# A second early SAGE sweep over three blocks with the late unit's own product made ahead, and a triangle product of the edge build replaced by sums of ranks on TensorE

## The chip, the cores and the metric

The kernel runs on one core of a Trainium2 chip, in one launch. The time is the device time of that core in microseconds (us). TensorE (PE) multiplies matrices into PSUM, VectorE (DVE) and ScalarE (ACT) work element by element, GpSimd (POOL) here mainly issues indirect DMAs, and SyncE (SP) issues the large DMAs. PEld is the loading of weights into TensorE, beside its matmuls. Lower is better.

## The reference

Four graph networks over the same 6250 nodes and 100000 edges (`src`, `dst`, sorted by `dst`), each with a residual and a layer norm. Cut to what matters:

```python
def aggregate(m, w): return segment_sum(m[src] * w[:, None], dst, 6250)

# L0: GCN, 3 layers, edge weights w and self loops, norm = dinv[src] * w * dinv[dst]
h = relu(gcn(x, W1, b1)); h = relu(gcn(h, W2, b2)); x = layernorm(x + gcn(h, W3, b3) @ Wl + bl)
# L1: SAGE, 2 layers: mean over the incoming edges
h = relu(x @ W1_self + mean_agg(x) @ W1_neigh + b1)
x = layernorm(x + h @ W2_self + mean_agg(h) @ W2_neigh + b2)
# L2: encoder, 5 steps of a GRU over aggregate(h @ conv_w[i], 1), decoder
x = layernorm(x + decoder(gru5(encoder(x))))
# L3: GCN with unit weights, 1 layer
x = layernorm(x + gcn(x, W, b))
```

## The kernel before

The kernel makes two dense adjacency matrices in HBM, source node by destination node (6272 x 6272): `W_adj` in float32 with the edge weights, for the first network, and `C_adj` in float16 with edge counts, for the others. Each aggregation is then a dense product of node features with such a matrix.

**Build** (`build_adjacency`). SP writes zeros over both matrices. The edges come in 49 batches of 2048 (16 tiles of 128). Two edges of one batch can be the same cell, so each batch is first merged: for each tile pair (j, i) with j <= i a 128x128 matrix `Eq` tells which edge of tile j has the key of which edge of tile i. DVE makes the `Eq` rows of the first 6 tiles (`compare_rows`, L474), ACT those of the other 10 from a squared distance and a Relu (`distance` L306, `equality` L314), each with the row sums in `total`. ACT also issues the loads of the batch's keys (`load_keys`, L291): the one for batch b+2 after its own rows of batch b, and after DVE's (`row_used`). DVE then makes one-hot matrices for the degrees (`one_hots`: L482, L487, L497) and `Et`, the diagonal blocks of `Eq` times a triangle (row <= column), in two halves (L495, L500). TensorE's `batch` waits for `equal_set` (the last of these) and `late_rows` (ACT's), multiplies all `Eq` blocks by the weights and a count (L554), each `Et` block by a column of ones (L557), and the one-hots (L560), and counts `batch_counted`. DVE's `merge` (L508 to L517) takes the sums from PSUM: an edge is the last of its cell if no equal one is at or after it (`total` minus the triangle's sum is 0); its target is the cell then, and a spare place otherwise. DVE's order is: compare rows of batch b+1, merge batch b, one-hots of batch b+1. POOL adds one tile per indirect DMA (`add_column`, L606), 784 for `W_adj` and then 784 for `C_adj`, in the batches' order, each batch after its `cell_set`.

**Layers** (`run_layers`). A stage (start, gcn 0 to 2, sage, enc, gru 0 to 3, out) aggregates the features it makes: 13 blocks of 512 destination nodes, in four sweeps over all 49 chunks of 128 source nodes. A sweep (first block, blocks, first PSUM bank) holds its blocks in PSUM banks, and for each chunk SP loads the matrix rows of these blocks into a ring of 8 slots (one more for chunk 0), up to 8 ahead of TensorE (`chunk_used`); `chunk` (L1049) multiplies one block after the other, in two passes either way (float32, or a high and a low half in float16). The start stage and gcn 2 take the blocks downwards, `DOWNWARD = ((9,4,0), (5,4,4), (1,4,0), (0,1,4))`, since the edges of the last blocks are added first. Before their last sweep, over block 0 alone, comes the head of the next stage's aggregation. For gcn 2 that is the sage stage with `EARLY_SWEEPS["sage"]`: of its first two sweeps the first 1 + 5 x 8 = 41 chunks (`early_parts`, `EARLY_LAPS`), whose source nodes are all outside unit 0. Their units (4 chunks each) have their dense part made as they come: `sage_products` (L1070 own, L1071 neighbour), `sage_unit` on DVE, `sage_turned` (L1080), with the PSUM banks of `SAGE_BANKS`. The late unit, unit 0, is made after gcn 2's last sweep, then the 8 remaining chunks of both sweeps follow, and the other two sweeps.

SP waits before sweep k of the start stage and of gcn 2 until the adds which that sweep's blocks need have landed (`ready`), and before their last sweep until all 784 of that matrix have (`adds_landed`); nothing queued on SP behind that wait is loaded sooner. This point is called the **gate** below, once for `W_adj` and once for `C_adj`. The lines for it are those in `sync` of `run_layers` under `if added:`.

## Time and profile before

| | us |
|---|---|
| median of 3 runs (5269.39 to 5279.17) | 5274.72 |
| the profiled execution, its own time | 5281.61 |
| its span, first to last instruction | 5279.8 |
| PE busy in the span | 4749.6 (90%) |
| POOL busy in the span | 2490.1 (47%) |
| the chain that ended last: PE / DVE / issue / DMA | 83% / 10% / 3% / 3% |

The build takes the first 988 us or so of the span and the layers the rest. In the build no engine is busy all the time on its own page line; what bounds it is read from one batch of the timeline. In the layers TensorE hardly ever waits. POOL's adds go on beside both until about 3021 us. The rows that the prediction reads are below, in groups.

### The profile page before, as it was taken

Reading aid. Unit: us, or ns where it says so; the run is one execution under the profiler, and the core shown is the slowest. Engines: PE = TensorE matmul, PEld = TensorE weight load, DVE = VectorE, ACT = ScalarE, POOL = GpSimd, SP = SyncE. Lnnn points to the kernel's source line nnn. Section 1 sums busy time; section 2 is a strip of 40 time slices with the busy share of each in tenths; the row PEclk is TensorE's granted clock in tenths of the full one; section 3 lists DMA queues with packets and bytes.
Section 4 is the critical chain, followed back from the end, with each engine's and each line's share of the span. In section 5 each row is a group of like instructions: output and inputs, shape, how many; then the busy total and the mean of one; then the engine's idle time right before and its main releaser. Section 6 shows DMA issues by size and latency. Waiting matters only on the chain.

```text
span 5279.8 us, 74661 instructions
## 1 busy us (share of the span) xinstructions
PE 4749.6 (90%) x25659; PEld 2552.1 (48%) x25659; DVE 1671.3 (32%) x3025; ACT 1364.8 (26%) x2522; POOL 2490.1 (47%) x1708
## 2 busy tenths in 40 slices
PE   3555555799999999999999999999999999999999
PEld 3555555444444444444455444544444444444444
DVE  9999999400000000110051103203022030220642
ACT  7898998300000111111120002102011020110410
POOL 4788888888888888888888700000000000000100
PEclk7665555799999999999999999999999999999999
DMA  9999998599999999999999986785866858768477
GB/s 327 342 340 340 329 338 217 138 309 307 289 279 293 291 297 287 287 279 299 257 253 274 265 302 195 233 284 163 292 216 217 287 168 282 229 205 287 141 238 249
DMA packets 792328, 1402.59 MB, mean 266 GB/s; under 512 B 268308, under 2 KB 513000, under 8 KB 760808
## 3 DMA queue, kind: packets, MB, share of 16 engines
q1 hardware_dynamic: 552012, 1342.89, 76.9%
q0 software_dynamic: 225792, 0.70, 7.9%
q10 hardware_dynamic: 14364, 56.99, 2.9%
q8 instruction: 84, 1.38, 0.1%
q14 instruction: 76, 0.62, 0.0%
HBM read 1160.09 MB, written 240.26 MB: 265 GB/s over the span
## 4 chain that ended last, share of the span: by engine, by line
PE 83%; DVE 10%; issue 3%; DMA 3%; ACT 0%; SPq 0%; ACTq 0%; DVEq 0%
PE psum L1049 66%; DVE arena L474 5%; PE psum L560 3%; DMA arena<-W_adj 2%; PE psum L554 2%; PE psum L997 2%; PE psum L999 2%; DVE arena L495 1%; PE psum L1004 1%; PE psum L1001 1%; DVE arena L500 1%; DVE arena L482 1%; DVE arena L497 1%; PE psum L1097 1%; PE psum L981 1%
## 5 line engine op out<-in xcount | busy, mean ns | idle before, releaser
L1049 PE MATMUL psum<-arena 128*128 128x512 f16 (+3 forms) x14014 | 3668.7, 422 | 18.5 <-DMA arena<-W_adj 10.4
L1049 PEld LDWEIGHTS psum<-arena 128*128 (+2 forms) x14014 | 1670.3, 123 | 1958.7 <-issue 866.2
L606 POOL DMA_INDIRECT W_adj<-arena x784 | 1216.1, 1551 | 272.3 <-issue 242.6
L606 POOL DMA_INDIRECT C_adj<-arena x784 | 1218.8, 1555 | 241.3 <-issue 241.3
L857 POOL TENSOR_TENSOR arena<-arena 128x512 f32 (+1 forms) x13 | 21.7, 1673 | 1693.3 <-DVE arena L1630 1693.3
L554 PE MATMUL psum<-arena 128*128 (+1 forms) x6664 | 226.4, 167 | 433.5 <-DVE arena L500 398.3
L474 DVE TENSOR_SCALAR_CACHE_REDUCE arena<-arena 128x2048 bf16<-128x2048 f32 (+5 forms) x294 | 572.0, 2007 | 0.0
L306 ACT ACTIVATE arena<-arena 128x1280 bf16<-128x1280 f32 (+4 forms) x490 | 426.7, 880 | 95.4 <-PE psum L560 45.1
L554 PEld LDWEIGHTS psum<-arena 128*128 128x128 bf16 x6664 | 215.1, 104 | 448.2 <-issue 401.3
L314 ACT ACTIVATE arena<-arena 128x1280 bf16<-128x1280 bf16 (+4 forms) x490 | 424.2, 866 | 0.0
L1892 DVE COPY arena<-psum 128x512 f32<-128x512 f32 (+1 forms) x39 | 23.2, 653 | 1009.9 <-PE psum L1097 1009.9
L560 PE MATMUL psum<-arena 128*128 128x98 f32 x1568 | 307.7, 386 | 2.0 <-issue 1.8
L1894 DVE TENSOR_SCALAR arena<-psum,arena 128x512 f32<-128x512 f32 (+1 forms) x31 | 22.2, 735 | 903.0 <-PE psum L1049 903.0
L560 PEld LDWEIGHTS psum<-arena 128*128 128x128 f32 x1568 | 300.6, 299 | 2.4 <-issue 2.3
L1547 ACT ACTIVATE arena<-psum,arena 128x512 f32<-128x512 f32 (+1 forms) x47 | 28.2, 650 | 931.7 <-PE psum L1049 931.7
L1527 ACT ACTIVATE arena<-arena 128x128 f32 x288 | 85.4, 308 | 516.1 <-PE psum L1049 502.3
L855 POOL COPY arena<-arena 128x512 f32 (+1 forms) x13 | 8.0, 616 | 326.2 <-DVE arena L1630 326.2
L997 PE MATMUL psum<-arena 128*128 (+1 forms) x260 | 137.4, 611 | 9.9 <-DVE arena L1901 5.9
L1516 ACT ACTIVATE arena<-arena 128x128 f32<-128x128 f32 x4 | 0.9, 297 | 546.9 <-DVE arena L1685 546.9
L999 PE MATMUL psum<-arena 128*128 (+1 forms) x260 | 134.5, 599 | 0.0
L1773 DVE SCALAR_TENSOR_TENSOR arena<-psum,arena 128x512 f32 (+1 forms) x48 | 36.0, 751 | 293.5 <-ACT arena L1426 293.5
L557 PE MATMUL psum<-arena 128*128 128x1 bf16 x784 | 126.0, 165 | 2.1 <-issue 2.1
(269 smaller groups left out, 2589.4 us busy)
## 6 DMA issues: line engine op xcount, KB each, us to landing
arena<-C_adj SPq DMA_DIRECT2D x653, 384.0 KB
arena<-C_adj SPq DMA_DIRECT2D x441, 512.0 KB
arena<-W_adj SPq DMA_DIRECT2D x196, 1024.0 KB
arena<-W_adj SPq DMA_DIRECT2D x163, 768.0 KB
arena<-C_adj SPq DMA_DIRECT2D x294, 288.0 KB
arena<-W_adj SPq DMA_DIRECT2D x98, 832.0 KB
W_adj<-arena SPq DMA_DIRECT2D x24, 3200.0 KB
W_adj<-arena SPq DMA_DIRECT2D x24, 3072.0 KB
```

The lines of the kernel that those rows point to most:

```text
L306: act.activation(apart[:, u % 2, 0:(TB - j) * P], krow[:, slot, j * P:], ACT.Square, bias=keyf[:, b * TB + j:b * TB + j + 1], scale=-1.0). ...
L314: act.activation(Eq[:, slot, at:at + (TB - j) * P], apart[:, u % 2, 0:(TB - j) * P], ACT.Relu, bias=one[:, 0:1], scale=-1.0, accum_out=tot ...
L474: ins = dve.tensor_scalar(Eq[:, slot, at:at + (TB - j) * P], krow[:, slot, j * P:], keyf[:, b * TB + j:b * TB + j + 1], None, ALU.is_equal ...
L482: dve.tensor_tensor(high, psRamp[:, 0:CHUNKS].unsqueeze(1).to_broadcast([P, TB, CHUNKS]), dhi[:, b * TB:(b + 1) * TB].unsqueeze(2).to_broa ...
L554: pe.matmul(psS[:, slot, 5 * i:5 * i + 4], Eq[:, slot, block_of(j, i)], V[:, ds(b * TB + j, 1), :].rearrange("p a c -> p (a c)"), start=(i ...
L557: pe.matmul(psS[:, slot, 5 * i + 4:5 * i + 5], Et[:, slot, own_at(i), :], ones[:, 0:1], start=False, stop=(i == TB - 1), skip_group_check= ...
L560: ins = pe.matmul(psD[:, 0:2 * CHUNKS], ohl[:, j, :], ohv[:, slot, j].rearrange("p c k -> p (c k)"), start=False, stop=False, skip_group_c ...
L606: return pool.indirect_dma_start(table, bass.IndirectOffsetOnAxis(idx[:, t:t + 1], 0), values[:, of:of + 1], None, compute_op=ALU.add)
L997: pe.matmul(psum[:, banks[gate], :], gates[:, gate * D:(gate + 1) * D], unit(fm, j), start=True, stop=False)
L999: pe.matmul(psum[:, banks[gate], :], wt[f"whhT{gate}"], unit(h_fm, j), start=False, stop=True).then_inc(s["probs_in"], 1)
L1049: ins = pe.matmul(psum[:, bank + b, 0:width], lhs, ring[:, slot, offset + b * BANK:offset + b * BANK + width], start=begin and part == 0, ...
L1527: act.activation(chunk32[:, u, :], h_nm[:, ds(i * LAP + (u + 1), 1), :].rearrange("p a f -> p (a f)"), ACT.Copy).then_inc(s["chunk_set"], 1)
```

## The change

**Build.** The triangle's product is gone: `psUpto`, `Et`, `own_at` and DVE's two multiplications L495 and L500 per batch. In place of the column of ones against `Et`, TensorE now multiplies the diagonal block of `Eq` itself by `rank` (two columns: ones, and a power of two that grows with the partition). The first sum counts the equal edges of the own tile, the second compares with `above`, 1.875 times the own power, which tells whether an equal edge stands later in the tile. DVE's merge gets one more operation of 16 columns (`later`), so `merged` counts 4 per batch, and its setup 7 small operations in place of one. `equal_set` is now signalled by the weighted one-hot.

**Early SAGE sweep.** The second early sweep goes over three blocks, 2 to 4, in banks 5 to 7, in place of two, 3 and 4, in banks 6 and 7; the stage's last sweep goes over two blocks in place of three. The late unit's own product (`late_product`, 4 matmuls) is made in the first early sweep, after chunk place 20, into bank 6; DVE copies it to `own_in`, the second early sweep waits for the copy (`late_kept`), and after the gate only the neighbour products of the late unit are left.

```diff
-SAGE_BANKS = (((0, 1, 2),), ((4, 5, 6),), ((5, 6, 7),), ((4, 5, 4),))
+SAGE_BANKS = (((0, 1, 2),), ((4, 5, 6),), ((5, 6, 7),), ((4, 6, 4),))
...
-EARLY_SWEEPS = {"gcn": ((5, 4, 0), (9, 4, 4), (2, 3, 0), (0, 2, 4)), "sage": ((5, 4, 0), (3, 2, 6), (9, 4, 0), (0, 3, 4))}
+EARLY_SWEEPS = {"gcn": ((5, 4, 0), (9, 4, 4), (2, 3, 0), (0, 2, 4)), "sage": ((5, 4, 0), (2, 3, 5), (9, 4, 0), (0, 2, 4))}
...
@@ build_adjacency: scalar
-                act.wait_ge(s["merged"], 3 * (b - 3) + 1)
+                act.wait_ge(s["merged"], 4 * (b - 3) + 1)
@@ build_adjacency: vector, setup
-        dve.memset(ones, 1.0)
+        dve.memset(rank[:, 0:1], 1.0)
...
-        link(dve.tensor_scalar(psUpto, ramp, pcol[:, 0:1], None, ALU.is_ge))
+        link(dve.tensor_copy(place[:, 0:1], pcol))
+        link(dve.tensor_scalar(place[:, 1:2], place[:, 0:1], 1, None, ALU.logical_shift_right))
+        link(dve.tensor_tensor(place[:, 0:1], place[:, 0:1], place[:, 1:2], ALU.add))
+        link(dve.tensor_scalar(place[:, 0:1], place[:, 0:1], float(RANK_LOW), None, ALU.add))
+        link(dve.tensor_scalar(power.bitcast(I32), place[:, 0:1], 23, None, ALU.logical_shift_left))
+        dve.tensor_copy(rank[:, 1:2], power)
+        link(dve.tensor_scalar(above, power, RANK_EDGE, None, ALU.mult))
@@ one_hots
-            dve.wait_ge(s["late_rows"], b * (TB - DVE_ROWS) + half - DVE_ROWS)
-            dve.tensor_tensor(Et[:, slot, 0:half, :], near, psUpto.unsqueeze(1).to_broadcast([P, half, P]), ALU.mult)
             dve.wait_ge(s["hot_set"], b + 1)
             dve.tensor_tensor(weighted, high, psW[:, b * TB:(b + 1) * TB].unsqueeze(2).to_broadcast([P, TB, CHUNKS]),
-                              ALU.mult)
-            dve.wait_ge(s["late_rows"], (b + 1) * (TB - DVE_ROWS))
-            dve.tensor_tensor(Et[:, slot, half:, :], far, psUpto.unsqueeze(1).to_broadcast([P, half, P]),
                               ALU.mult).then_inc(s["equal_set"], 1)
@@ merge
-            dve.tensor_scalar(mask, more, 0.0, -1.0, ALU.is_equal, ALU.mult).then_inc(s["merged"], 1)
+            dve.scalar_tensor_tensor(out=later, in0=sums[:, :, 5], scalar=above[:, 0:1], in1=more, op0=ALU.is_ge,
+                                     op1=ALU.add).then_inc(s["merged"], 1)
+            dve.wait_ge(s["merged"], 4 * b + 2)
+            dve.tensor_scalar(mask, later, 0.0, -1.0, ALU.is_equal, ALU.mult).then_inc(s["merged"], 1)
@@ build_adjacency: tensor
-                pe.matmul(psS[:, slot, 5 * i + 4:5 * i + 5], Et[:, slot, own_at(i), :], ones[:, 0:1],
+                pe.matmul(psS[:, slot, 6 * i + 4:6 * i + 6], Eq[:, slot, block_of(i, i)], rank,
                           start=False, stop=(i == TB - 1), skip_group_check=True)
@@ run_layers: tensor
+            def late_product(j, ahead):
+
+                pe.wait_ge(s["products_read"], ahead.read + early_units().index(j))
+                for c in range(UC):
+                    ins = pe.matmul(psum[:, sage_banks(j)[1], c * D:(c + 1) * D],
+                                    h_fm[:, j * BANK + c * P:j * BANK + (c + 1) * P], wt["W1s"], start=True, stop=True)
+                ins.then_inc(s["late_own"], 1)
...
                             if i_:
+                                pe.wait_ge(s["late_kept"], 1)
                                 pe.wait_ge(s["seconds_read"], ahead.seconds + early_units().index(units[-1]) + 1)
...
+                                if i_ == 0 and place == UC * (len(units) + 1):
+                                    late_product(early_units()[-1], ahead)
                                 early_spell(place, ahead, ("sage", 0), i_)
@@ run_layers: vector, sage_unit and gcn 2
+                if j in early_units_of(SPLIT):
+                    own = own_in[:, 0].rearrange("p (c f) -> p c f", f=D)
+                    dve.wait_ge(s["late_kept"], 1)
...
+                        if sweep == SPLIT:
+                            dve.wait_ge(s["late_own"], 1)
+                            dve.tensor_copy(own_in[:, 0], psum[:, sage_banks(early_units()[-1])[1], :]) \
+                                .then_inc(s["late_kept"], 1)
```

How the instructions stand in the program, first on DVE in the build: the end of a batch's comparisons, the merge of the batch before, the one-hots, and the next comparison. Before:

```order
L474 TENSOR_SCALAR arena<-arena 128x1408
L508 TENSOR_REDUCE arena<-psum 128x16
L509 CAST arena<-psum 128x16
L510 SCALAR_TENSOR_TENSOR arena<-psum,arena 128x16
L513 TENSOR_SCALAR arena<-arena 128x16
L515 TENSOR_TENSOR arena<-arena 128x16
L517 TENSOR_TENSOR arena<-arena 128x16
L482 TENSOR_TENSOR arena<-psum,arena 128x16x49
L487 TENSOR_TENSOR arena<-psum,arena 128x2048
L495 TENSOR_TENSOR arena<-arena,psum 128x1024
L497 TENSOR_TENSOR arena<-arena,psum 128x16x49
L500 TENSOR_TENSOR arena<-arena,psum 128x1024
```

The same place in the changed kernel, where lines are numbered anew (L478 is the comparison, L508 the new operation, L486, L491 and L495 the one-hots):

```order
L478 TENSOR_SCALAR arena<-arena 128x1408
L503 TENSOR_REDUCE arena<-psum 128x16
L504 CAST arena<-psum 128x16
L505 SCALAR_TENSOR_TENSOR arena<-psum,arena 128x16
L508 SCALAR_TENSOR_TENSOR arena<-psum,arena 128x16
L511 TENSOR_SCALAR arena<-arena 128x16
L513 TENSOR_TENSOR arena<-arena 128x16
L515 TENSOR_TENSOR arena<-arena 128x16
L486 TENSOR_TENSOR arena<-psum,arena 128x16x49
L491 TENSOR_TENSOR arena<-psum,arena 128x2048
L495 TENSOR_TENSOR arena<-arena,psum 128x16x49
```

The two operations of 1024 columns are gone and one of 16 columns came. Next, TensorE from the fourth unit of the early SAGE work to the first chunks after the gate. Before (L1049 is `chunk`, L1070 and L1071 own and neighbour product, L1080 the transposes):

```order
L1080 MATMUL psum<-arena 128x128 x4
L1049 MATMUL psum<-arena 128x512 x462
L1070 MATMUL psum<-arena 128x128
L1071 MATMUL psum<-arena 128x128
L1070 MATMUL psum<-arena 128x128
L1071 MATMUL psum<-arena 128x128
L1070 MATMUL psum<-arena 128x128
L1071 MATMUL psum<-arena 128x128
L1070 MATMUL psum<-arena 128x128
L1071 MATMUL psum<-arena 128x128
L1049 MATMUL psum<-arena 128x512 x32
```

In the changed kernel (L1047 is `chunk`, L1077 the late unit's own product, L1070 the neighbour product, L1087 the transposes):

```order
L1087 MATMUL psum<-arena 128x128 x4
L1047 MATMUL psum<-arena 128x512 x32
L1077 MATMUL psum<-arena 128x128 x4
L1047 MATMUL psum<-arena 128x512 x512
L1070 MATMUL psum<-arena 128x128 x4
L1047 MATMUL psum<-arena 128x512 x32
L1087 MATMUL psum<-arena 128x128 x4
```

Between the last transposes of the early units and the late unit's neighbour product stand 544 chunk matmuls where 462 stood, 82 more, and the own product moved up among them. Last, SP over the same stretch, before:

```order
L898 DMA arena<-C_adj 128x2048 x41
L898 DMA arena<-C_adj 128x1024 x41
L881 DMA arena<-C_adj 128x512
L934 DMA arena<-C_adj 128x3x512 x16
L881 DMA arena<-C_adj 128x2048 x8
```

and in the changed kernel:

```order
L896 DMA arena<-C_adj 128x2048 x41
L896 DMA arena<-C_adj 128x1536 x41
L879 DMA arena<-C_adj 128x512
L932 DMA arena<-C_adj 128x3x512 x16
L879 DMA arena<-C_adj 128x2048 x8
```

The 41 loads ahead of the gate carry three blocks in place of two. The gate is SP's wait ahead of the load of 512 columns.

## Rows read from the trace of the kernel before

**Rows 1.** The page: TensorE's busy tenths in 40 slices of the span.

```profile
PE   3555555799999999999999999999999999999999
```

**Rows 2.** Timeline of one batch: start, us, engine, line, operation, idle before and releaser.

```profile
417.45 2.34 DVE L474 TENSOR_SCALAR_CACHE_REDUCE arena<-arena 128x2048 bf16<-128x2048 f32 x1
...
423.01 5.62 PE L560 MATMUL psum<-arena 128*128 128x98 f32 x32
...
429.04 0.20 DVE L508 TENSOR_REDUCE arena<-psum 128x16 f32<-128x48 f32 x1
...
435.05 1.21 DVE L500 TENSOR_TENSOR arena<-arena,psum 128x1024 bf16<-128x1024 bf16 x1
...
436.18 2.34 DVE L474 TENSOR_SCALAR_CACHE_REDUCE arena<-arena 128x2048 bf16<-128x2048 f32 x1
...
436.65 0.18 PE L554 MATMUL psum<-arena 128*128 x1 [8.03 <-DVE arena L500]
```

**Rows 3.** View of line L474: durations in ns, first and last start.

```profile
L474 DVE TENSOR_SCALAR_CACHE_REDUCE arena<-arena x294: 1669/2008/2348, 28.4 to 965.5; 128x2048 bf16<-128x2048 f32 x49, 128x1792 bf16<-128x1792 f32 x49, 128x1536 bf16<-128x1536 f32 x49
```

**Rows 4.** Waits from 300 to 900 us: us in total, times, longest.

```profile
PE psum L554 <- DVE arena L500: 242.0, 31, 8.2
```

**Rows 5.** Timeline of ACT: first rows of batches 1 and 2.

```profile
40.54 2.51 ACT L306 ACTIVATE arena<-arena 128x1280 bf16<-128x1280 f32 x2 [3.63 <-DVE arena L474]
...
58.70 2.51 ACT L306 ACTIVATE arena<-arena 128x1280 bf16<-128x1280 f32 x2 [0.54 <-ACT arena L314]
```

**Rows 6.** Timeline: TensorE's end of the build and first chunks of the layers.

```profile
980.02 6.94 PE L560 MATMUL psum<-arena 128*128 128x98 f32 x32
...
995.35 15.17 PE L1049 MATMUL psum<-arena 128*128 128x512 f32 x35 [4.89 <-ACT arena L1436]
...
999.75 0.34 PEld L1049 LDWEIGHTS psum<-arena 128*128 128x128 f32 x1 [0.52 <-issue]
...
1001.11 0.19 PEld L1049 LDWEIGHTS psum<-arena 128*128 128x128 f32 x1 [0.24 <-issue]
```

**Rows 7.** Timelines of POOL, TensorE and SP about the gate of W_adj.

```profile
1551.65 1.55 POOL L606 DMA_INDIRECT W_adj<-arena  x1 [0.30 <-issue]
...
1555.01 114.32 PE L1049 MATMUL psum<-arena 128*128 128x512 f32 x266
...
1600.28 0.37 SPq L881 DMA_DIRECT2D arena<-W_adj  x1
```

**Rows 8.** Timelines of the same engines about the gate of C_adj.

```profile
2979.70 73.33 PE L1049 MATMUL psum<-arena 128*128 128x512 f16 x339
...
3019.43 1.56 POOL L606 DMA_INDIRECT C_adj<-arena  x1 [0.30 <-issue]
...
3025.44 0.36 SPq L881 DMA_DIRECT2D arena<-C_adj  x1
...
3053.72 0.49 PE L1070 MATMUL psum<-arena 128*128 128x128 f32 x2 [0.69 <-ACT arena L1547]
...
3055.60 0.59 PE L1049 MATMUL psum<-arena 128*128 128x512 f16 x2
```

**Rows 9.** Timeline of POOL: the start of batch 2's adds.

```profile
141.55 0.19 POOL L580 TENSOR_TENSOR arena<-arena 128x1 f32<-128x1 f32 x1 [14.02 <-issue]
```

**Rows 10.** DMA issues by transfer: KB each, median us from issue to landing.

```profile
keys<-arena ACTq DMA_DIRECT2D x1, 392.0 KB, 2.3
...
W_adj<-arena SPq DMA_DIRECT2D x1, 16.0 KB, 5.2
```

**Rows 11.** Timeline of ACT at the end of the sage stage.

```profile
3209.86 1.26 ACT L1547 ACTIVATE arena<-psum,arena 128x512 f32<-128x512 f32 x2 [62.19 <-PE psum L1049]
```

**Rows 12.** Timeline of SP: loads of the second early sweep, two blocks each.

```profile
2999.97 25.36 SPq L898 DMA_DIRECT2D arena<-C_adj  x30
```

**Rows 13.** POOL's adds by line, from 300 to 900 us and from 1600 to 3000 us.

```profile
L606 POOL DMA_INDIRECT W_adj<-arena x319 | 493.8, 1548 | 101.9 <-issue 98.3 <-DMA W_adj<-arena 3.4 <-DVE arena L517 0.2
...
L606 POOL DMA_INDIRECT C_adj<-arena x746 | 1159.4, 1554 | 230.1 <-issue 230.1
```

More of the change, by code:

```diff
@@ L44 @@
 ZONES = 36
+RANK_LOW = 32
+RANK_EDGE = 1.875
 ZONE = 256
@@ L190, in build_adjacency @@
     psD = psum[:, 3, :]
-    psRamp, psUpto = psum[:, 2, 0:P], psum[:, 2, P:2 * P]
+    psRamp = psum[:, 2, 0:P]
     psW = psum[:, 4:6, :].rearrange("p a b -> p (a b)")[:, 0:TILES]
@@ L212, in build_adjacency @@
     V = take(P, [TILES, 4], BF16)
-    ones, one = take(P, [16], BF16), take(P, [8], F32)
+    rank, one = take(P, [2], BF16), take(P, [8], F32)
+    power, above, place = take(P, [1], F32), take(P, [1], F32), take(P, [2], I32)
     ramp = take(P, [P], F32)
@@ L216, in build_adjacency @@
     krow = take(P, [2, B], F32)
-    Et = take(P, [2, TB, P], BF16)
     ohl, ohv = take(P, [TB, P], F32), take(P, [2, TB, 2, CHUNKS], F32)
-    total, more = take(P, [3, TB], F32), take(P, [TB], F32)
+    total, more, later = take(P, [3, TB], F32), take(P, [TB], F32), take(P, [TB], F32)
     apart = take(P, [2, (TB - DVE_ROWS) * P], BF16)
@@ L505, in merge @@
             dve.wait_ge(s["batch_counted"], b + 1)
-            sums = psS[:, slot, 0:TB * 5].rearrange("p (i c) -> p i c", c=5)
+            sums = psS[:, slot, 0:TB * 6].rearrange("p (i c) -> p i c", c=6)
             at = slice(b * TB, (b + 1) * TB)
@@ L531, in vector @@
         dve.wait_ge(s["ramps"], 7 + SPLIT)
-        dve.tensor_copy(ones, ones).then_inc(built, 1)
+        dve.tensor_copy(rank, rank).then_inc(built, 1)
     def tensor(pe):
@@ L789, in run_layers @@
             "sum_dve sum_act hi_set var_set std_set gates_set pre_set new_set unit_set kept dve_step " \
-            "dve_stage act_stage abs_set reach_in reach_set probs_in probs_set " \
+            "late_own late_kept dve_stage act_stage abs_set reach_in reach_set probs_in probs_set " \
             "enc_in enc_set enc_out enc_kept parts_in " \
```

16 lines of the change are left out of this document (6 added, 10 removed).

## The prediction

> **What bounds the kernel now.** The page's line of busy tenths comes first: from the ninth slice on TensorE is busy nine tenths or more [rows 1], so the layers are bound by TensorE, and only the build, before it, and places where TensorE comes to wait can give time. I then read one batch of the build in the timeline. From DVE's first comparison at 417.45 to the next one at 436.18 are 18.7 us without a gap, and TensorE stands for 8.0 us until L500 ends [rows 2]. Comparisons run from the first at 28.4 to the last at 965.5, and the last of a batch starts some 10 us after its first: 927 us for 48 batches, 19.3 us a batch [rows 3]. DVE bounds the build, with TensorE close beside it: its idle time is 242.0 us in 31 batches or 7.8 us each [rows 4], so it works 11.5 us of 19.3.
>
> The third thing to read is a clock of its own. POOL's adds go at one pace from the start of batch 2 at 141.55 [rows 9] to the last at 3019.43 [rows 8], and neither DVE's work nor TensorE's sets them. All of `W_adj` must have landed before the start stage's last sweep and all of `C_adj` before gcn 2's. SP got past the first gate at 1600.28, 47 us after POOL's last add of `W_adj` ended at 1553.2 [rows 7], and past the second at 3025.44, 4.4 us after the last add ended at 3020.99 [rows 8]. So the first gate has room, and the second has nearly none. Whatever is won in the build reaches the second gate and stops there, unless other work stands ahead of it. That is how I price the change.
>
> **The build.** Removed: L495 and L500, 1.21 us each (the row is of L500, and the other has its shape) [rows 2]. Added: one operation of 16 columns, which I take at the 0.2 us of L508 [rows 2]. DVE's own turn falls from 18.7 to 18.7 - 2.4 + 0.2 = 16.5 us. Next is the turn through TensorE: 11.5 us of matmuls, 0.5 us from DVE's signal to the first of them (436.18 to 436.65), and DVE's part outside the comparisons, which was 436.18 - 429.04 = 7.1 and becomes 4.9 us [rows 2]: 16.9 us. But late is now ACT. It makes ten rows of each batch and sends for keys in between, and at the start, where nobody held it, batch 1 to batch 2 took 58.70 - 40.54 = 18.16 us with only its own work before it [rows 5]. In the kernel before that was hidden under 19.3. So the batch falls to 18.2 and not to 16.9. ACT's chain: 40.5 + 47 x 18.16 = 894.0 for its start of batch 48, with a later start of some 1 us (seven small setup operations on DVE ahead of the first comparison) against 1 us for the two key loads that the last batches lack. Its rows take 18.16 - 0.54 = 17.6, TensorE's batch then 11.5 to 12: 923.5, where it was 980.02 + 6.94 = 986.96 [rows 6]. The build ends **63 us** sooner. The ends are 0 (the removed operations hidden after all) and 48 x (19.3 - 16.9) = 115 us. I take 63 since it comes from a row in which ACT runs alone. TensorE's matmuls cost nothing new: as many, two columns wide for one, on weights of the same size. The keys come denser by 6%, beside SP's zeros; POOL's batch 2 waits for zeroed cells [rows 9], and for one more key load of 1 MB ahead of it I allow 1 us on the whole of POOL's stream, 0 to 3 as the range.
>
> **From the build to the second gate.** Start stage and gcn stages hold the same work and start at 995.35 - 63 = 932. At the first gate SP arrives at 1537, before the adds have landed, and waits some 18 us. TensorE would begin its last sweep at 1669.33 - 98 x 0.43 = 1627.2 before (49 chunks of two records in the row of 266 [rows 7]), thus at 1564 now; a load issued at about 1555 lands in 2.3 us, or 5.2 at the most [rows 10]. TensorE hardly waits, but it has lost the lead of its ring. Some us may go there, and they cost nothing as long as the second gate is still shut.
>
> At the second gate TensorE began gcn 2's last sweep at 3053.03 - 98 x 0.2163 = 3031.8 (98 of the 339 records in 73.33 us [rows 8]). Ahead of it now stand 41 x 2 = 82 matmuls more, 82 x 0.2163 = **17.7 us**, and the late unit's own product, half of the 1.9 us from 3053.72 to 3055.60 in which both products ran [rows 8]: 0.9 us. TensorE gets there at 3031.8 - 63 + 17.7 + 0.9 = 2987. The added waits `late_own` and `late_kept` hold nothing: DVE has finished its units by then, its copy is one operation of 512 columns, and TensorE has 21 chunks of work until it needs it; behind DVE's wait stands only the sum of that sweep.
>
> The gate opens between 3021.0 (POOL's last add issued) and 3025.4 (SP had passed) [rows 8]. I take 3024, as the adds have still to be made in memory, and 1 us for POOL's later start. SP's issue and its landing take 0.4 and 2.3 us [rows 8, 10]: TensorE starts at **3027.7** after 40 us of idleness. The same point of work lay at 3031.8 + 17.7 + 0.9 = 3050.4 before. Won: 22.7 us.
>
> **Behind the gate.** TensorE resumes at its lower clock: in rows 6 a weight load follows every 0.86 us at 999.75 and every 0.43 us at 1001.11, so from 995.35 it ran 5 us at 1.2 GHz and lost 2.6 us after a wait. I take 3 us, with the empty ring in it; the range is 2.5 to 10. The stage's last sweep has two blocks, so ACT scales one sum there and not two in 1.26 us before the next stage can begin [rows 11]: 0.6 us won. The 82 matmuls come off that sweep (98 of them) and 16 go to the remaining chunks; the sum of work is the same.
>
> **The sum:** 22.7 - 3 + 0.6 = 20.3 us. Against the profiled execution's own 5281.61 that is 5261.3. It lay 6.9 us above the median of the runs, 5274.7, which gives 5254.4: I say **5254 us**.
>
> A rule of the Trainium skill speaks of POOL's stream. The trace first: an add takes 1548 ns in the build, with both removed operations running, and 1554 ns from 1600 to 3000 us, where DVE is nearly idle [rows 13]. "SBUF — State Buffer", section "Who interferes with whom", says that VectorE and GpSimd share a port pair, and that a GpSimd DMA's descriptors wait while DVE holds it. By that rule fewer DVE operations would open the gate sooner; by the rows DVE cost POOL nothing, and the same page exempts an operation with one input in SBUF. The sum keeps 3024.
>
> **The rivals.**
> (a) *The gate does not bind, the build's gain is small.* It decides below 22.7 us of gain at the gate, a batch above 18.8 us; or with over 40 us lost at the first gate with the emptied ring. At 19.0 us a batch the gain is about 13, less little, so 5262. Against it: ACT's 18.16 and 40 us in hand.
> (b) *The two-block sweep is starved.* SP would need 1.3 us for each 256 KB, as in a three-block sweep of six matmuls at 0.2163; decides above 1.27 us a load: 49 x (1.3 - 0.865) = 21 us lost, the gain gone, 5275. Against it: 30 such loads in 25.36 us, 0.85 each, TensorE fed, with POOL's adds beside them [rows 8, 12].
> (c) *Slower: the clock stays low.* After 40 us without work TensorE runs at 1.2 GHz and, fed chunk by chunk from an empty ring, does not get back. Each us of full-speed work costs one more. It decides above 23.3 + 10.5 = 34 us of such work, that is through gcn 2's last sweep (21.2 us) and the 8 four-block chunks behind it (64 x 0.2163 = 13.8). With the three-block ones too (10.4) it is 45 us: 5281.6 - 23.3 + 45 = 5303, at the median 5296. Against it: 5 us in rows 6, also from an empty ring.
> (d) *POOL's stream ends sooner*, the Trainium skill's rule as a mechanism here: adds that waited behind L495 and L500, up to 49 x 2.4 = 119 us. Then TensorE at 2987 binds, 63 + 0.6 us are won: 5211. Against it: rows 13.
>
> **How the numbers follow.** Forecast 0.80, with 12 to 28 us won: 22.7 + 3 + 0.6 and 1 to 2 more at its best, 22.7 - 1.4 (gate at 3025.4) - 2.9 (landing 5.2) - 2 (POOL) - 5 (clock) and so 12 at its worst. (a) 0.08, (b) 0.04, (c) 0.04, (d) 0.04. The runs shown differ by 5 us from their median; the range is 5243 to 5267, and leaves out (b), (c), (d) and parts of the edges. A measurement can tell about 0.2%, 10.5 us. Faster by more: 0.80 + 0.06 of (a) + (d) = 0.90. Within it: 0.06, from (a) and (b). Slower: 0.04.
>
> **What the profile after would show.** The batches every 18.2 us, ACT without idle time but for its key loads, and TensorE waiting for ACT's L-line of `equality` and not for DVE. The first chunk near 932. SP idle at the first gate until about 1555 and TensorE not. One wait of TensorE near 2987 to 3028, ended by a load of `C_adj`, and a granted clock of half for about 5 us behind it. POOL's last add within 3 us of 3019.4. Wrong it would be if that last add moved by more than 10 us, if TensorE did not wait at the second gate, or if the idle time moved to another stage.

## The result, and the profile after

The changed kernel takes 5256.93 us (median of 8 runs, 5255.05 to 5263.43) against 5274.27 us for the kernel before (8 runs beside it, 5269.39 to 5279.17): a ratio of 0.9967 with a 95% interval of 0.9957 to 0.9976. The forecast was 5254 us, its range 5243 to 5267. Its profiled execution took 5257.21 us by its own time, 5255.4 us of it the span.

The build first. These are TensorE's waits over the whole of after (us in total, times, longest), its last three batches of the build, and the first chunk of the layers; below them DVE's comparison line with its first and last start.

```profile
PE psum L552 <- ACT arena L312: 324.1, 42, 8.5
...
882.73 5.93 PE L558 MATMUL psum<-arena 128*128 128x98 f32 x32
...
900.91 7.04 PE L558 MATMUL psum<-arena 128*128 128x98 f32 x32
...
918.44 6.81 PE L558 MATMUL psum<-arena 128*128 128x98 f32 x32
...
934.28 36.16 PE L1047 MATMUL psum<-arena 128*128 128x512 f32 x96 [4.65 <-ACT arena L1446]
...
L478 DVE TENSOR_SCALAR_CACHE_REDUCE arena<-arena x294: 1668/2006/2347, 28.8 to 904.0; 128x2048 bf16<-128x2048 f32 x49, 128x1792 bf16<-128x1792 f32 x49, 128x1536 bf16<-128x1536 f32 x49
```

TensorE waits for ACT's L312 (`equality`, L314 before) where it waited for DVE's L500 [rows 4]. A batch takes 900.91 - 882.73 = 18.2 us, the last one, whose ACT part has no keys to send for, 17.5. The build ends at 925.25 where it ended at 986.96 [rows 6], and the layers begin 61 us sooner.

Now the second gate, in the timelines of TensorE, SP and POOL of after:

```profile
2939.81 45.49 PE L1047 MATMUL psum<-arena 128*128 128x512 f16 x210
...
3019.71 1.56 POOL L604 DMA_INDIRECT C_adj<-arena  x1 [0.30 <-issue]
...
3022.66 0.33 SPq L879 DMA_DIRECT2D arena<-C_adj  x1
...
3024.73 1.03 PE L1047 MATMUL psum<-arena 128*128 128x512 f16 x2 [39.43 <-DMA arena<-C_adj]
3026.80 22.85 PE L1047 MATMUL psum<-arena 128*128 128x512 f16 x96 [1.04 <-DMA arena<-C_adj]
```

POOL's last add comes at 3019.71, where it came at 3019.43 [rows 8]. TensorE is there at 2985.3, stands idle for 39.4 us, and ends gcn 2's last sweep at 3049.65; before it ended at 3053.03. So of 61 us, 3.4 are left here, and the rest of the gain is work that no longer stands behind this point: 82 matmuls and the late unit's own product. At the sage stage's end the two kernels are 22.5 us apart (ACT's last scaling of a sum at 3187.38, 3209.86 in rows 11, one in place of two):

```profile
3187.38 0.69 ACT L1557 ACTIVATE arena<-psum,arena 128x512 f32<-128x512 f32 x1 [41.04 <-PE psum L1047]
```

This reads as the forecast had it. The experiments show that two of its terms were nevertheless wrong.

### The profile page after: what moved, and what is told of

Read it like the earlier page. It is cut to its first block, busy times and chain, and to the rows that moved or that the text cites. A ratio compares the mean times of both kernels' runs of the same rounds, so it can differ in the third digit from the quotient of the medians.

```text
span 5255.4 us, 74620 instructions
## 1 busy us (share of the span) xinstructions
PE 4736.0 (90%) x25659; PEld 2544.5 (48%) x25659; DVE 1574.6 (30%) x2983; ACT 1364.6 (26%) x2522; POOL 2486.5 (47%) x1708
## 4 chain that ended last, share of the span: by engine, by line
PE 42%; POOL 30%; issue 8%; DVE 0%; POOLq 0%; DMA 0%; ACT 0%; ACTq 0%; SPq 0%; DVEq 0%
PE psum L1047 33%; POOL C_adj L604 22%; POOL W_adj L604 8%; PE psum L995 2%; PE psum L997 2%; PE psum L1002 1%; PE psum L999 1%; PE psum L1027 0%; POOLq L598 0%; POOL arena L578 0%; PE psum L975 0%; PE psum L1142 0%; PE psum L1158 0%; PE psum L979 0%; PE psum L1138 0%
## 5 line engine op out<-in xcount | busy, mean ns | idle before, releaser
L1047 PE MATMUL psum<-arena 128*128 128x512 f16 (+3 forms) x14014 | 3670.3, 422 | 55.0 <-DMA arena<-C_adj 40.5
L1047 PEld LDWEIGHTS psum<-arena 128*128 (+2 forms) x14014 | 1670.5, 123 | 1996.2 <-issue 867.5
L604 POOL DMA_INDIRECT W_adj<-arena x784 | 1214.3, 1549 | 273.9 <-issue 245.4
L604 POOL DMA_INDIRECT C_adj<-arena x784 | 1216.8, 1552 | 241.7 <-issue 241.7
L478 DVE TENSOR_SCALAR_CACHE_REDUCE arena<-arena 128x2048 bf16<-128x2048 f32 (+5 forms) x294 | 571.9, 2006 | 0.0
L552 PE MATMUL psum<-arena 128*128 (+1 forms) x6664 | 211.1, 166 | 388.4 <-ACT arena L312 324.1
L312 ACT ACTIVATE arena<-arena 128x1280 bf16<-128x1280 bf16 (+4 forms) x490 | 424.2, 866 | 0.0
L995 PE MATMUL psum<-arena 128*128 (+1 forms) x260 | 137.6, 611 | 9.9 <-DVE arena L1918 5.9
L997 PE MATMUL psum<-arena 128*128 (+1 forms) x260 | 134.6, 599 | 0.0
L555 PE MATMUL psum<-arena 128*128 128x2 bf16 x784 | 126.0, 165 | 0.0
```

Source lines behind the costliest of these rows:

```text
L312: act.activation(Eq[:, slot, at:at + (TB - j) * P], apart[:, u % 2, 0:(TB - j) * P], ACT.Relu, bias=one[:, 0:1], scale=-1.0, accum_out=tot ...
L478: ins = dve.tensor_scalar(Eq[:, slot, at:at + (TB - j) * P], krow[:, slot, j * P:], keyf[:, b * TB + j:b * TB + j + 1], None, ALU.is_equal ...
L552: pe.matmul(psS[:, slot, 6 * i:6 * i + 4], Eq[:, slot, block_of(j, i)], V[:, ds(b * TB + j, 1), :].rearrange("p a c -> p (a c)"), start=(i ...
L555: pe.matmul(psS[:, slot, 6 * i + 4:6 * i + 6], Eq[:, slot, block_of(i, i)], rank, start=False, stop=(i == TB - 1), skip_group_check=True)
L604: return pool.indirect_dma_start(table, bass.IndirectOffsetOnAxis(idx[:, t:t + 1], 0), values[:, of:of + 1], None, compute_op=ALU.add)
L995: pe.matmul(psum[:, banks[gate], :], gates[:, gate * D:(gate + 1) * D], unit(fm, j), start=True, stop=False)
```

## The experiments

In the runs below L604, L605, L606, L609 and L616 are the line of POOL's adds, and L1047 to L1067 that of the sweeps' matmuls. "Last add" is the start of the last add into `C_adj`.

### The two halves apart (e1_build, e2_sweep)

e1_build is the kernel before with the rank sums alone:

```diff
-            dve.tensor_tensor(Et[:, slot, 0:half, :], near, psUpto..., ALU.mult)
...
-            dve.tensor_tensor(Et[:, slot, half:, :], far, psUpto..., ALU.mult)
...
-                pe.matmul(psS[:, slot, 5 * i + 4:5 * i + 5], Et[:, slot, own_at(i), :], ones[:, 0:1],
+                pe.matmul(psS[:, slot, 6 * i + 4:6 * i + 6], Eq[:, slot, block_of(i, i)], rank,
...
+            dve.scalar_tensor_tensor(out=later, in0=sums[:, :, 5], scalar=above[:, 0:1], in1=more, ...)
```

> The kernel before with the rank sums in the build alone; the early sage sweep, the last sweep and the late unit stay as before. Second gate (the stream of adds is a clock of its own, and the wait for the last add into C_adj binds): the build's last matmul comes about 62 us sooner (925 us in place of 987), TensorE then waits at the last sweep of gcn 2 for about 60 us in place of next to none, the last chunks start with the adds at 3020 to 3025 us, and the whole is won by the old slack alone: 3 to 5 us, about 5270 us. Rival (the build's gain passes): 60 us less, about 5212 us. Rival (the small sums matter, no gate): anything between, with no wait of TensorE at C_adj.

e2_sweep is the kernel before with the sweep and the late product alone:

```diff
-..."sage": ((5, 4, 0), (3, 2, 6), (9, 4, 0), (0, 3, 4))}
+..."sage": ((5, 4, 0), (2, 3, 5), (9, 4, 0), (0, 2, 4))}
...
+            def late_product(j, ahead):
...
+                                if i_ == 0 and place == UC * (len(units) + 1):
+                                    late_product(early_units()[-1], ahead)
```

> The kernel before with the second early sage sweep over three blocks and the late unit's own product made ahead; the build stays as before. Second gate: TensorE reaches the last sweep of gcn 2 about 18 us later than before, after the adds have landed, so that nothing is waited for there, and the moved work is merely done earlier: 0 to 2 us won (5272 to 5275 us), the same time. Rival (the reordering is worth something by itself, for example shorter chains at the sage stage's end): 10 us or more. The two halves alone then add up to 3 to 7 us where the change as a whole won 17 to 24.

Measured: e1_build 5281.16 us (11 runs, ratio to before 1.0013, 1.0004 to 1.0022); e2_sweep 5255.3 us (6 runs, ratio 0.9966, 0.9954 to 0.9978). Both expectations missed. The build's half was to win 3 to 5 us and wins nothing: its median lies 5.6 us above that of before beside it. The rival by which its gain passes the gate is refuted, since TensorE waits there for 56.9 us (about 60 expected). The sweep's half wins the whole 20 us by itself, and I had expected 0 to 2. Both expectations stood on the forecast's second sentence on the gate, that TensorE came there at 3031.8 with nearly no room. TensorE at the gate, in e1_build and in e2_sweep:

```profile
3022.96 1.04 PE L1047 MATMUL psum<-arena 128*128 128x512 f16 x2 [56.86 <-DMA arena<-C_adj]
...
3021.92 1.03 PE L1049 MATMUL psum<-arena 128*128 128x512 f16 x2 [13.11 <-DMA arena<-C_adj]
```

e2_sweep has the build of before and 18.6 us more work ahead of the gate, and yet TensorE comes there 23 us sooner than before's profile shows, and waits. So the profile of before was perhaps not what the kernel usually does. (e2_sweep holds both the three-block sweep and the late unit's own product; no run separates the two, 17.7 and 0.9 us in the prediction's sum.)

### A second profile of before (e7_before), and shifted code (e6_shift)

> The kernel before once more, unchanged, for a second profile. If the 81 gaps of TensorE in the build (34.5 us) belong to the program, they are there again and the build ends at 987 us; if they belong to one execution, the build ends about 40 us sooner, TensorE waits 25 to 30 us at C_adj, and the whole is 3 to 5 us shorter than the first profiled run's 5281.6.

e6_shift:

```diff
+SHIFT = 16
...
         pe.transpose(psR, needed, ident[0:NB, 0:NB]).then_inc(s["needed_turned"], 1)
+        for _ in range(SHIFT):
+            pe.wait_ge(s["needed_set"], 2)
```

> The kernel before with 16 waits that are already met put on TensorE's queue ahead of the build's loop; nothing else is changed, and the place of every later instruction of TensorE in its instruction memory is. It asks why the same code of the build took TensorE to 987 us in the profiled run of before and to about 948 us in e2_sweep. If the place of the loop's instructions does it, the idle time of TensorE put down to issue in the build (34.5 us in 81 gaps before, 2.4 us in e2_sweep) changes with the shift, and the build ends up to 40 us sooner; by the second gate the whole then stays within 5 us of before (5270 to 5280), since TensorE only waits longer at C_adj. If it is something else, the profile shows the 81 gaps again.

The waits of TensorE and DVE from 0 to 1000 us, first in the profile that the forecast used, then in e7_before, the same kernel:

```profile
PE psum L554 <- DVE arena L500: 398.3, 48, 26.5
PE psum L554 <- issue: 34.5, 81, 7.6
...
DVE arena L508 <- PE psum L560: 21.3, 26, 1.9
```

```profile
PE psum L554 <- DVE arena L500: 425.7, 49, 26.5
...
DVE arena L508 <- PE psum L560: 13.8, 3, 11.4
```

In the first execution TensorE's stream of small matmuls had 81 gaps that no semaphore explains, so that in 26 batches DVE waited for TensorE. DVE stands idle for 27 of the 937 us from 28 to 965 there, and for 8 of the 915 us from 28 to 943 in e7_before. In e7_before the gaps are absent but for one, DVE's last comparison starts at 943.9 and not at 965.5 [rows 3], and this is the end of the build, the first chunk, and the gate:

```profile
957.37 6.74 PE L560 MATMUL psum<-arena 128*128 128x98 f32 x32
...
972.70 30.46 PE L1049 MATMUL psum<-arena 128*128 128x512 f32 x80 [5.03 <-ACT arena L1436]
...
3016.82 1.56 POOL L606 DMA_INDIRECT C_adj<-arena  x1 [0.30 <-issue]
...
3021.91 1.04 PE L1049 MATMUL psum<-arena 128*128 128x512 f16 x2 [14.94 <-DMA arena<-C_adj]
3023.71 23.31 PE L1049 MATMUL psum<-arena 128*128 128x512 f16 x96 [0.76 <-DMA arena<-C_adj]
```

The build ends at 964.11, 22.9 us sooner than in rows 6, and the kernel before waits at the second gate too, 14.9 us (17.1 in e6_shift, whose build ends at 965.4). e6_shift takes 5272.33 us, a ratio of 0.9997 (0.9988 to 1.0006). The gaps are absent with the code in its old place, with it shifted, and in e2_sweep; they belonged to one execution. What made them is open. The expectation for e7_before had the direction right and the sizes not: the build was to end some 40 us sooner and TensorE to wait 25 to 30 us. The expectation for e6_shift took e2_sweep's build to end at about 948 us; the trace has 964.04. The change's own gain in the build is then 964.11 - 925.25 = 38.9 us, not 61.7.

It also shows how e2_sweep could win alone. The room at the gate in the kernel before is 15 to 17 us, and the moved work is 18.6. Its build ends at 964.04, as in e7_before, but TensorE waited for loads in the start stage's first sweep for only 0.9 us, against 9.4 (the 26 small matmuls behind its first sweep start at 1113.26 and at 1128.37 in e7_before), so that TensorE still had 13.1 us left. In an execution like e7_before it would come 3 to 4 us late, and that is what the build's half would be worth there; only in one as disturbed as the first profile, where TensorE came at 3031.8, would it be more. The medians of e2_sweep (5255.3) and of after (5256.9, 5254.1) don't show it.

### The stream delayed (e4_delay), and cut short (e5_fewer)

```diff
+DELAY = 80
...
     def gpsimd(pool):
+        for i in range(DELAY):
+            waited(pool, pool_tick, ticked, NB + i)
         for b in range(NB):
...
-            waited(pool, pool_tick, ticked, NB + b)
+            waited(pool, pool_tick, ticked, NB + DELAY + b)
```

> The kernel after with 80 small additions of one column put on GpSimd between the last add into W_adj and the first into C_adj, each waiting for the one before: a pure delay of the stream, read in the trace as the shift of the last add into C_adj (an unknown 15 to 40 us). Second gate: TensorE's wait at C_adj grows by the same amount and the whole ends later by the same, to within 1 us. Rival (the stream has slack, other work sets the end): the last add is later, the whole is not, 5257 us.

POOL's delay, the first add behind it, the last add, and TensorE at the gate, in e4_delay:

```profile
1557.54 22.51 POOL L579 TENSOR_TENSOR arena<-arena 128x1 f32<-128x1 f32 x81
1580.19 1.55 POOL L605 DMA_INDIRECT C_adj<-arena  x1
...
3045.66 1.56 POOL L605 DMA_INDIRECT C_adj<-arena  x1 [0.30 <-issue]
...
3050.78 1.04 PE L1050 MATMUL psum<-arena 128*128 128x512 f16 x2 [64.27 <-DMA arena<-C_adj]
```

The last add is 25.95 us later than in after, TensorE's wait 24.84 us longer, the profiled execution's own time (5282.34) 25.1 us longer. The median is 5280.76 (11 runs, ratio to before 1.0011, 1.0002 to 1.0020), 24 us above after's. The stream's delay passes into the whole one for one, as expected.

e5_fewer leaves the last two batches of adds into `C_adj` out, 30 adds of 784, so its counts of edges lack them, and lets SP's gate for `C_adj` wait for 30 fewer:

```diff
+LEFT_OUT = 2
...
-        for b in range(NB):
+        for b in range(NB - LEFT_OUT):
             if b:
                 pool.wait_ge(c_added[(b - 1) % 2], batch_before(pool, flight, flight_set, b))
...
-                    least = [adds_landed(u) for u in range(2)]
+                    least = [adds_landed(u) - 16 * tiles_of(NB - 1 - u) * (k > 0) for u in range(2)]
```

> The kernel after with the last two batches of adds into C_adj left out (30 of 784; the counts of edges then lack them, so the output is not the reference's). Second gate: the stream ends 30 x 1.855 = 55.7 us sooner, about 2964 us, which is ahead of TensorE's arrival at 2985.3; TensorE no longer waits there, and the whole is shorter by TensorE's idle time in the kernel after (39.4 + 1.0 us) and by about 2 to 3 us of low clock behind it: about 42 us, 5214 us, and not by the whole 55.7 us. This is all that the build's gain of 62 us could ever bring here. Rival (the adds are not what holds the end): unchanged, 5257 us. Rival (something else, such as the loads, is late next): 10 to 30 us less with a wait of TensorE on C_adj left.

Measured: 5214.79 us (4 runs, ratio to before 0.9890, 0.9875 to 0.9905), 42 us below after, as expected. TensorE's sweeps, the last add, and SP's first load behind the gate:

```profile
2939.68 60.81 PE L1048 MATMUL psum<-arena 128*128 128x512 f16 x281
...
2962.79 1.55 POOL L605 DMA_INDIRECT C_adj<-arena  x1 [0.30 <-issue]
...
2969.46 0.36 SPq L880 DMA_DIRECT2D arena<-C_adj  x1
...
3002.18 7.07 PE L1048 MATMUL psum<-arena 128*128 128x512 f16 x32
```

The stream ends 56.9 us sooner, TensorE runs through without a wait, and the whole gains about what TensorE had stood idle (39.4 + 1.0) plus its low clock (2 to 3 in the expectation), not the 56.9. So the gate held 42 us of after's time and no more.

### Another order of the batches (e3_order)

```diff
-ORDER = [NB - 1] + [t - d for t in range(NB - 2, 8, -4) for d in (1, 3, 0, 2)] + [7, 5, 2, 4, 1, 6, 3, 0]
+ORDER = [NB - 1, NB - 2, NB - 3] + [t - d for t in range(NB - 4, 12, -4) for d in (1, 3, 0, 2)] + [8, 6, 9, 7, 4, 2, 5, 1, 3, 0]
```

> The kernel after with another order of the batches (the first three run down one by one, then groups of four), so that the zeroed parts of W_adj that batches 1 and 2 of the adds wait for are ready sooner. Second gate: the 25 us that the stream of adds loses to those two waits (9.4 and 15.7 us) shrink, the last add into C_adj issues 10 to 20 us sooner than 3019.7, TensorE's wait at the gate shrinks from 39 us by as much, and the whole ends sooner by the same: 5237 to 5247 us. Rival (the stream's start does not matter, the gate is set by something else, such as the landing of the adds): the last add is sooner but the first load from C_adj is not, 5257 us. Rival (the new order makes each add or its batch's release slower, since neighbours in time now share rows): no gain or a loss.

Measured: 5262.24 us (11 runs, ratio to before 0.9975, 0.9966 to 0.9984), where 5237 to 5247 were expected: no gain over after. POOL's waits before batches 1 and 2 of `W_adj` and before batches 1 and 2 of `C_adj`, and its last add:

```profile
92.62 0.19 POOL L578 TENSOR_TENSOR arena<-arena 128x1 f32<-128x1 f32 x1 [5.71 <-DMA W_adj<-arena]
...
128.06 0.19 POOL L578 TENSOR_TENSOR arena<-arena 128x1 f32<-128x1 f32 x1 [5.55 <-DMA W_adj<-arena]
...
1576.59 0.19 POOL L578 TENSOR_TENSOR arena<-arena 128x1 f32<-128x1 f32 x1 [3.79 <-DMA C_adj<-arena]
...
1613.87 0.19 POOL L578 TENSOR_TENSOR arena<-arena 128x1 f32<-128x1 f32 x1 [7.60 <-DMA C_adj<-arena]
...
3021.16 1.56 POOL L604 DMA_INDIRECT C_adj<-arena  x1 [0.30 <-issue]
```

The waits before batches 1 and 2 of `W_adj` (9.35 and 15.71 us in after), which I put down to rows not yet zeroed, fell to 5.71 and 5.55. These end with an add's landing, that is, they now wait for the batch before, since neighbours in this order share rows. The first add into `C_adj` came at 1543.45 (1555.21 in after). But the same order is used for `C_adj`, where nothing waits for zeros, and there the two new waits gave 11.4 us back. The expectation priced the `W_adj` half of the stream and forgot that the same table orders the `C_adj` half. The last add was 1.5 us later than in after and the median 5.3 us; only part of the latter is in the last add, and the rest is not explained. So this run doesn't contradict the gate; the edit did not do what I had in mind.

### The order mended (e9_orders, e12_orders)

The same order for `W_adj`, and for the first five batches of `C_adj` one whose neighbours lie apart, with the waits between neighbours worked out for it (`flight_c`). SP's gates ahead of the last one in gcn 2 also wait for the first four batches, the ones that changed places:

```diff
+C_FIRST = (0, 2, 3, 1, 4)
...
-                add_column(pool, C_adj, idx, cnt, b * TB + j).then_inc(c_added[b % 2], 16)
+                at_ = C_FIRST[b] if b < len(C_FIRST) else b
+                add_column(pool, C_adj, idx, cnt, at_ * TB + j).then_inc(c_added[b % 2], 16)
...
+                        if k and sweep < SPLIT:
+                            sp.wait_ge(added[u], AHEAD + 2 * PER_BATCH)
```

> The kernel after with the adds into W_adj in the order of e3_order (whose first add into C_adj came at 1543.5 us against 1555.2 us in the kernel after) and the adds into C_adj in an order whose neighbours share no rows (e3_order lost 3.8 and 7.6 us there to waits for the batch before). Second gate, and the adds ahead of it the clock: the last add into C_adj at 3006 to 3010 us, the first chunk behind the gate 5.1 us later as in every run so far, the whole 2237.5 to 2240 us behind the last add: 5244 to 5249 us, and TensorE's wait at C_adj 27 to 30 us in place of 39. Rival (the stream has a pace of its own that gives such gains back, as in e3_order): last add at 3017 to 3021, 5255 to 5261 us.

> The kernel of e9_orders once more, timed in rounds, with a second profile: whether it beats the kernel after by the 9 to 12 us that its last add is sooner, or by the 3.6 us between the medians of the last call (5250.5 against 5254.1). If the time is the last add into C_adj plus 2236 to 2238 us, the profiled run fits that again; a median at 5244 to 5248 us makes the gain 8 us or more, one at 5249 to 5253 us about 5 us.

Measured: e9_orders 5250.54 us (5 runs, ratio to before 0.9955, 0.9941 to 0.9969); e12_orders, the same kernel again, 5246.57 us (5 runs, 0.9951, 0.9937 to 0.9964). The last add and the gate in e9_orders, then in e12_orders:

```profile
3007.95 1.56 POOL L616 DMA_INDIRECT C_adj<-arena  x1 [0.30 <-issue]
...
3013.01 1.03 PE L1067 MATMUL psum<-arena 128*128 128x512 f16 x2 [41.31 <-DMA arena<-C_adj]
```

```profile
3000.10 1.56 POOL L616 DMA_INDIRECT C_adj<-arena  x1 [0.30 <-issue]
...
3005.25 1.03 PE L1067 MATMUL psum<-arena 128*128 128x512 f16 x2 [24.42 <-DMA arena<-C_adj]
```

The last add is 9 to 20 us sooner than in after, and the profiled executions took 5244.22 and 5238.42 us. Each is the fastest of its five runs, so the medians say more of what the order wins. Over its ten runs the median is 5248.2, over after's thirteen 5256.0: 7.8 us less, the fastest of the kernels here that leave nothing out. Their runs overlap (5238 to 5256 against 5253 to 5263), and they were timed side by side only once, where the medians stand at 5250.5 and 5254.1, 3.6 us apart. The last add in e9_orders came where it was expected (3006 to 3010), but two things missed: the median lies above the 5244 to 5249 us expected, and TensorE's wait did not shrink to 27 to 30 us in e9_orders. TensorE came to the gate sooner too, at 2971.7.

### Repeats (e10_after, e8_build, e11_build)

> The kernel after once more, beside the others of this call, with a second profile. If the time is the last add into C_adj plus a constant, the profiled run lies 2237 to 2239 us behind its last add; the median 5254 to 5260 us.

> The kernel of e1_build once more, for a second profile: how far the time of the last add into C_adj (3017.9 us) moves from one execution to the next, and whether the 5 us that e1_build's median lies above before's come from there (last add at 3022 to 3026 us) or from the low clock behind TensorE's wait.

> The kernel of e1_build once more, timed in rounds: whether it is really slower than the kernel before (5281.2 against 5275.6 us in the first call), although its two profiled runs were 5276.7 and 5271.7 us. If the time is the last add into C_adj plus a constant (2257 to 2259 us without the early sweep), the median is 5272 to 5278 us, the same as before within 0.1%; if the longer wait of TensorE costs something that the two profiles do not show, it is again 4 to 6 us above before.

e10_after: 5254.14 us (5 runs, ratio to before 0.9961, 0.9947 to 0.9974). e8_build, one run: 5271.68. e11_build: 5277.94 us (11 runs, 1.0006, 0.9997 to 1.0015). The first and the last median lie at the inner edges of their expected ranges. e8_build's last add came at 3014.43, so what e1_build's median lies above before's does not show in it as a later add. Every profiled execution, with its last add beside its own time:

| profiled execution | early sage sweep of three blocks | last add | wait at the gate | own time | own time less last add |
|---|---|---|---|---|---|
| before, first profile | no | 3019.43 | none | 5281.61 | 2262.2 |
| e7_before | no | 3016.82 | 14.9 | 5275.51 | 2258.7 |
| e6_shift | no | 3018.73 | 17.1 | 5276.67 | 2257.9 |
| e1_build | no | 3017.87 | 56.9 | 5276.68 | 2258.8 |
| e8_build | no | 3014.43 | 59.2 | 5271.68 | 2257.3 |
| e11_build | no | 3014.03 | 57.1 | 5272.42 | 2258.4 |
| e2_sweep | yes | 3016.82 | 13.1 | 5255.57 | 2238.8 |
| after | yes | 3019.71 | 39.4 | 5257.21 | 2237.5 |
| e10_after | yes | 3016.84 | 42.8 | 5254.14 | 2237.3 |
| e3_order | yes | 3021.16 | 39.0 | 5261.18 | 2240.0 |
| e4_delay | yes | 3045.66 | 64.3 | 5282.34 | 2236.7 |
| e9_orders | yes | 3007.95 | 41.3 | 5244.22 | 2236.3 |
| e12_orders | yes | 3000.10 | 24.4 | 5238.42 | 2238.3 |
| e5_fewer | yes | 2962.79 | none | 5210.83 | 2248.0 |

Where TensorE waits, the time is the last add plus a constant: 2257.3 to 2258.8 without the early sweep (mean 2258.2), 2236.3 to 2240.0 with it (mean 2237.8). The length of the wait, 13 to 64 us, is not in it. The two constants are 20.4 us apart, and that is what the change won in the profiled executions. The medians say 17.3 us for after, 20.7 for e10_after and 20.3 for e2_sweep, each against before beside it. Where TensorE does not wait, the rule fails in the direction it must (the first and the last row).

What stays open is e1_build. Its medians, 5281.2 and 5277.9, lie above those of before, the first with an interval that leaves 1 out, although its three profiled executions took 5271.7 to 5276.7 us. Their last adds are no later than before's. If it is a little slower, its three profiles don't show why: they caught quick executions, the second fastest of eleven in e1_build and the third of eleven in e11_build. The same holds for the table as a whole. Its rule is shown for profiled executions, and not for the other runs, whose last adds nobody saw.

## Why the prediction was right, and where it was not

**What bounds.** Right, and shown both ways: the stream of adds is a clock of its own, and the second gate takes what is won ahead of it (e4_delay, e5_fewer, e9_orders, e12_orders).

**The build's size.** The mechanism was right: ACT's turn of 18.16 us [rows 5] became the pace, 18.2 in after, and TensorE's wait is for ACT's L312. But "DVE bounds the build ... 19.3 us a batch" was the failing step. The rows showed DVE's turn as 18.7 without a gap [rows 2] and the mean as 19.3 [rows 3], and I took the mean as the kernel's pace without asking where 0.6 us a batch went. They went into TensorE's gaps of that one execution. In e7_before the last comparison starts at 943.9, which by the same sum makes 18.9 us a batch. The 63 us forecast met 61.7 on the same disturbed profile, and it is 38.9 against the undisturbed one. At the gate this did no harm, since 38.9 us are more than the room there too.

**The first gate.** Right: TensorE had no wait of more than 1.1 us there in after, and SP loaded from 1556.37 on (about 1555 forecast).

**The arrival at the second gate** was forecast at 2987 and was 2985.3 in after. That "the second has nearly none" of room was true of the one execution only: e7_before waits 14.9 us there. So **22.7 us won at the gate** had a term that was none: 3031.8 - 3027.7 = 4.1 us of former lateness. And **3 us for the low clock** were no cost of the change either. The stretch exists: in after the granted clock is half and then full:

```profile
3024.00:3031.00 7.00, 5.23 (x13) 0.51 0.97 310
3031.00:3050.00 19.00, 18.65 (x87) 1.00 0.74 248
```

The columns are the stretch, its length, TensorE's busy time, granted clock, DMA share and GB/s. TensorE had stood idle for 39.4 us; then it ran at 1.2 GHz for some 6 us and after that at 2.4 GHz. The sweep's 98 matmuls took 24.9 us from 3024.73 in place of 98 x 0.2163 = 21.2. But e7_before took 25.1 us for the same 98 from 3021.91, behind its own wait. The two false terms, +4.1 and -3, nearly cancelled, by luck.

**What was really won** can be read between e7_before and e10_after, whose last adds are 0.02 us apart and whose own times are 21.4. ACT's last scaling and the first matmuls of the next stage, in e7_before, then in e10_after:

```profile
3203.33 1.27 ACT L1547 ACTIVATE arena<-psum,arena 128x512 f32<-128x512 f32 x2 [62.19 <-PE psum L1049]
...
3206.07 0.72 PE L977 MATMUL psum<-arena 128*128 128x128 f32 x2 [2.78 <-ACT arena L1389]
3206.58 0.63 PE L981 MATMUL psum<-arena 128*128 128x128 f32 x2
```

```profile
3184.36 0.69 ACT L1557 ACTIVATE arena<-psum,arena 128x512 f32<-128x512 f32 x1 [41.04 <-PE psum L1047]
...
3186.53 0.46 PE L975 MATMUL psum<-arena 128*128 128x128 f32 x2 [2.20 <-ACT arena L1399]
3186.82 0.39 PE L979 MATMUL psum<-arena 128*128 128x128 f32 x2
```

The last scaling starts 19.0 us sooner (forecast 17.7 + 0.9 = 18.6), the next stage's first matmul 19.5 us (the one scaling less, forecast 0.6), and its first small matmuls are shorter, 0.39 for 0.63 us a pair, as TensorE is not at its low clock there. This holds over all profiles but one: with the early sweep of three blocks TensorE is idle for 2.20 us there and the pair takes 0.39 us in all eight, without it TensorE is idle for 2.78 us and the pair takes 0.63 to 0.64 us in five of six. The exception is e8_build (0.39 us behind 2.78), whose row in the table has the least of the five constants. So this term is shown, but it does not come in every execution. Three us of each in the view of windows, e7_before and then e10_after (busy time, granted clock, DMA share, GB/s):

```profile
3206.00:3209.00 3.00, 2.93 (x14) 0.52 0.51 208
```

```profile
3187.00:3190.00 3.00, 3.00 (x29) 1.00 1.02 419
```

It is 1.2 GHz in the one and 2.4 GHz in the other. By the start of the next stage but one (3488.30 in e10_after, 3509.43 in e7_before) the distance is 21.1 us. This last term, 1.6 us, was not foreseen. The sum would have been 18.6 + 0.6 + 1.6 = 20.8, and the table's means give 20.4. Forecast 20.3.

**From the sum to the time.** Taken off the profiled execution's 5281.61, 20.3 us give 5261.3; its row in the table is 4 us above the constant, and its last add is 2.6 us later than e7_before's. Subtracting the distance to the median, 6.9 us, took that out and gave 5254. Measured: 5256.9, and 5254.1 in e10_after. Part of this hit is luck as well. Between the two profiled executions themselves, before and after, lie 5281.61 - 5257.21 = 24.4 us and not 20.3: TensorE went on at 3024.73, where the forecast had 3027.7. And after's profiled execution lies only 0.3 us above its median.

**The rivals.** (a) fell: the gate binds, in every profile of the change that had all its adds. (b) fell: e2_sweep wins its 20 us with the three-block sweep. (c) fell, the clock was back after 6 us. (d) fell. An add takes 1547 ns from 300 to 900 us in after against 1548 [rows 13], and e1_build, which has only the two operations less on DVE, has its last adds at 3014.0 to 3017.9 against 3016.8 and 3019.4: 2 to 3 us at most, within what one execution differs from the next. By the Trainium skill's "SBUF — State Buffer", section "Who interferes with whom", a GpSimd DMA's descriptors wait while VectorE holds their shared port pair. The rows show no such wait to be relieved, which agrees with that section's exemption of an operation with one input in SBUF, outside VectorE's two-port modes: L495 and L500 read one input from SBUF and one from PSUM.

## What to carry to other kernels

Where a stream on another engine ends at a fixed time and the main engine must wait for its last item, price a change by what it moves across that point, and count a faster lead-in as nothing; here the build's half could have been left out at no loss that the medians show. The other half, the work moved ahead of the gate, won all of it. Before a sum rests on how much room there is at such a gate, compare the turn of one batch (18.7 us here) with the mean over all of them (19.3): where the mean is longer, look for what the difference is, and if it is idle time without a releaser, ask for a second profile. And when a table that sets an order is edited, go through every stream that reads it.

## What the runs showed of the hardware

One execution had 81 gaps, 34.5 us in all, in TensorE's stream of small matmuls, with no semaphore as their cause; in the thirteen other profiles TensorE has at most three such gaps in the build, 7.8 us together. Its time less its last add lies only some 4 us above e7_before's, because the gate took most of it: TensorE came there 24.8 us later (3031.8 against 3006.97), of which 14.9 us were room, and it did not fall to the low clock, which cost e7_before 3.9 us on the 98 matmuls. POOL's stream is steadier: from its first add into `C_adj` to its last it takes 1461.0 to 1468.4 us in the twelve profiles with all adds that keep neighbours apart there, and 1477.7 in e3_order. The first chunk behind the gate began 5.0 to 5.2 us after the last add in each of the twelve profiles in which TensorE waited.
